# Value products two key tiles at a time, projections between them, in a fused attention and feed-forward kernel

## The reference

```python
x = x + tanh(g_xattn[0]) * linear_attention(layernorm(x), ctx)      # 16 heads of 8
x = x + tanh(g_ffn[0])   * quantised_ffn(layernorm(x))              # 128 -> 512 -> 128
x = x + tanh(g_xattn[1]) * softmax_attention(layernorm(x), ctx)     # 16 heads of 8
x = x + tanh(g_ffn[1])   * experts(layernorm(x))                    # best 2 of 8
...
scores = jnp.einsum('bhqd,bhkd->bhqk', qh, kh) / jnp.sqrt(jnp.float32(D_K))
attn = jax.nn.softmax(scores, axis=-1)
context = jnp.einsum('bhqk,bhkd->bhqd', attn, vh)
...
h = jax.nn.gelu(jnp.einsum('bsd,fed,bske->bskf', x, w1, oh) + b1)
```

## Time and profile before

| | |
|---|---|
| median of 3 runs | 747.04 us (745.25 to 748.69) |
| profiled execution, its own time | 745.49 us |
| its span, first to last instruction | 743.7 us |
| TensorE busy | 665.1 us (89%) |
| VectorE busy | 520.3 us (70%) |
| ScalarE busy | 513.1 us (69%) |
| GpSimd busy | 269.6 us (36%) |

### The profile page before, as it was taken

How to read it: one execution, slowest core, us unless ns; L and a number is a source line. 1 busy time by engine, 2 the same in 40 slices (tenths; PEclk the granted TensorE clock), 3 DMA queues, 4 the chain that set the end, 5 groups by cost and what they waited for, 6 DMA issues and landing times.

```text
span 743.7 us, 19382 instructions
## 1 busy us (share of the span) xinstructions
PE 665.1 (89%) x7302; PEld 467.0 (63%) x7315; DVE 520.3 (70%) x1236; ACT 513.1 (69%) x839; POOL 269.6 (36%) x324
## 2 busy tenths in 40 slices
PE   3499999986468999999999999999999986999997
PEld 3488888874225665666665666566666664577777
DVE  5788989888778779878978878878876751212112
ACT  4488888876326887887787787787887866634441
POOL 4299999992243214304322422432233100000000
PEclk9899999999589999999999999999999999799999
DMA  4122223345523476356537636644664480211110
GB/s 145 41 84 84 83 87 111 111 142 31 121 73 84 98 167 139 95 129 135 130 91 148 149 91 143 135 110 110 135 157 114 86 192 9 60 29 58 29 42 26
DMA packets 59379, 74.42 MB, mean 100 GB/s; under 512 B 35320, under 2 KB 40178, under 8 KB 59306
## 3 DMA queue, kind: packets, MB, share of 16 engines
q1 hardware_dynamic: 59306, 73.39, 41.8%
HBM read 32.35 MB, written 1.40 MB: 45 GB/s over the span
## 4 chain that ended last, share of the span: by engine, by line
PE 43%; DVE 16%; issue 7%; ACT 2%; POOL 2%; SPq 1%; another core or an unknown queue 1%; DMA 1%; DVEq 0%; POOLq 0%; ACTq 0%
DVE mx L1615 8%; PE ps L662 8%; PE ps L750 7%; PE ps L811 7%; PE ps L823 7%; PE ps L737 6%; PE ps L648 4%; PE ps L654 2%; DVE kvall L1446 2%; ACT P L1023 1%; PE ps L684 1%; DVE amax L1485 1%; POOL KP L1134 1%; DVE silu L1530 1%
## 5 line engine op out<-in xcount | busy, mean ns | idle before, releaser
L1023 ACT ACTIVATE P<-ps,kbias,kscale 125x896 f32<-125x896 f32 x192 | 210.3, 1098 | 86.0 <-PE ps L737 83.0
L1615 DVE TENSOR_REDUCE mx<-ps 128x1 f32<-128x500 f32 x336 | 214.0, 671 | 46.6 <-PE ps L662 44.8
L662 PE MATMUL ps<-KP,Qb 128*128 128x500 bf16 x336 | 128.9, 386 | 16.4 <-DVE mx L1615 10.3
L1134 POOL TENSOR_TENSOR KP<-kvall,KP 128x1500 bf16<-128x1500 f32 x16 | 48.6, 3036 | 230.6 <-ACT KP L966 230.6
L750 PE MATMUL ps<-P,Vp 125*32 125x112 f32 x3072 | 113.5, 265 | 2.8 <-ACT P L1023 1.5
L750 PEld LDWEIGHTS ps<-P,Vp 125*32 125x32 f32 x3072 | 67.4, 109 | 53.1 <-issue 37.8
L533 PE MATMUL ps<-wkv,cT 128*125 128x256 f32 x384 | 91.8, 383 | 1.1 <-ACT arena L901 1.1
L533 PEld LDWEIGHTS ps<-wkv,cT 128*125 128x125 f32 x384 | 69.3, 190 | 10.1 <-issue 1.4
L1084 ACT ACTIVATE arena<-ps,b 128x448 f32<-128x448 f32 x64 | 40.4, 633 | 47.4 <-PE ps L811 41.5
L737 PE MATMUL ps<-QS,KS 128*128 128x112 bf16 x768 | 68.8, 215 | 2.4 <-DVE QS L1621 1.4
L737 PEld LDWEIGHTS ps<-QS,KS 128*128 128x128 bf16 x768 | 55.0, 99 | 23.3 <-issue 3.9
(11 more groups left out here) (216 smaller groups left out, 1007.4 us busy)
## 6 DMA issues: line engine op xcount, KB each, us to landing
cT<-ctxT_dram SPq DMA_DIRECT2D x32, 750.0 KB, 4.2
KS<-KP SPq DMA_DIRECT2D x48, 375.0 KB, 7.3
arena<-KP SPq DMA_DIRECT2D x48, 375.0 KB, 7.2
QS<-QD SPq DMA_DIRECT2D x96, 28.0 KB, 5.7
wgu<-w_dram SPq DMA_DIRECT2D x8, 256.0 KB, 3.2
silu<-w_dram SPq DMA_DIRECT2D x8, 256.0 KB, 2.9
x<-xh_dram SPq DMA_DIRECT2D x1, 512.0 KB, 3.6
mixed<-att SPq DMA_DIRECT2D x16, 28.0 KB
```

The costliest lines, as they stand in the source:

```text
L662: ins = nc.tensor.matmul(ps[:, bank, 0:KCW], q[:, 128 * c:128 * c + 128], KP[par][0][:, KCW * k:KCW * k + KCW], start=True, stop=True)
L1023: nc.scalar.activation(P[t % 2][0:TK, :].rearrange("p (k n) -> p k n", k=2), src, ACT.Exp, scale=kscale[0:TK, bass.ds(n, 1)], bias=kbias[0 ...
L1134: nc.gpsimd.tensor_tensor(KP[par][2][:], krest, KP[par][1][:], ALU.subtract).then_inc(sem("kp3_ready"), 1)
L1615: ins = v.tensor_reduce(mx[:, c, k:k + 1], ps[:, bank, 0:KCW], AX.X, ALU.max)
```

## The change

Value products are put off and done for two key tiles together in even tiles (tiles 10 and 11 in the next window's tile 0), except in the last window. The exponentials have four buffers, two of them in a part of `arena` that the first phase has left free. The large projections stand in odd tiles, the small units in even ones. VectorE's steps hang on other MX units; `gate` moves into the next window. At the end, `up` goes over the first half of the rows first, and its first four products and seven of the eight gating products stand between OT, FT, FO and ET.

```diff
+PAT = 6016
 PLACES = [
-    [[["MX0"], ["Q1"], ["MX1"]], [["MX2"], [], ["AT", "MX3"]], [["MX4"], ["OT"], ["MX5"]],
...
+    [[["MX0"], ["Q1"], ["MX1"]], [["MX2"], ["V0"], ["MX3"]], [["MX4"], ["AT"], ["MX5"]],
...
+TOGETHER = 2
...
-        P = [sb(f"P{n}", [128, HQ]) for n in range(2)]
+        P = [sb(f"P{n}", [128, HQ])[:] for n in range(2)]
+        P += [arena[:, PAT + HQ * n:PAT + HQ * n + HQ] for n in range(2)]
...
+                apart = fixed(i) and w == B - 1
...
-                    if t > 0:
+                    if t == 0:
+                        if not first:
+                            for before in range(T - TOGETHER, T):
+                                weigh(w - 1, 1 - par, before, first_pair)
+                    elif apart:
                         weigh(w, par, t - 1, first_pair)
-                    elif not first:
-                        weigh(w - 1, 1 - par, T - 1, first_pair)
+                    elif t % TOGETHER == 0:
+                        for before in range(t - TOGETHER, t):
+                            weigh(w, par, before, first_pair)
...
+            def up(e, par, first, of=range(8)):
+
+                xv = xT[:].rearrange("p (b q) -> p b q", q=HALF)
+                for u in of:
+                    k, c = divmod(u, FC)
...
+            pe.wait_ge(sem("side_free"), emptied((NT - 1, 1), "ET"))
+            up(0, 0, True, range(0, 1))
             fill(AFTER, "OT", B - 1, 1)
-            for unit in LAST:
-                fill(AFTER, unit, NT - 1, 1)
-
-
+            up(0, 0, True, range(1, 2))
+            fill(AFTER, "FT", NT - 1, 1)
+            logits(range(0, 3))
+            fill(AFTER, "FO", NT - 1, 1)
+            up(0, 0, True, range(2, 4))
+            logits(range(3, NT - 1))
+            fill(AFTER, "ET", NT - 1, 1)
             pe.wait_ge(sem("side_free"), emptied(AFTER, "ET"))
...
+            logits(range(NT - 1, NT)).then_inc(sem("logit_ps"), 1)
...
+                    elif par == 0 and k == 0:
+                        pe.wait_ge(sem("logit_ready"), 1)
...
-                if not (first and t < 2):
-                    act.wait_ge(sem("pv_done"), n - 1)
+                if not (first and t < 4):
+                    act.wait_ge(sem("pv_done"), n - 3)
...
-                for unit, later in (("K0", REST_LATER), ("K1", REST_LATER), ("Q1", 2)):
+                for unit, later in (("K0", REST_LATER), ("K1", REST_LATER), ("Q1", 1)):
...
-                        elif unit == "SH":
-                            gate(at, n)
...
-                        if unit == "U":
+                        if unit == "MX0":
+                            gate(prev(at), n)
+                        elif unit == "U":
...
-            lg = ps[:, 6, 0:NT * E].rearrange("p (t e) -> p t e", e=E)
+            lg = ps[:, 4, 0:NT * E].rearrange("p (t e) -> p t e", e=E)
```

More of the change, by code:

```diff
@@ L790, in _ @@
             weigh(B - 1, 1, T - 1, False)
[L791 to L812 removed]
+            def up(e, par, first, of=range(8)):
+                xv = xT[:].rearrange("p (b q) -> p b q", q=HALF)
+                for u in of:
+                    k, c = divmod(u, FC)
+                    if u == 0:
+                        pe.wait_ge(sem(f"w1_in{par}"), loads(e, par))
+                    if not (first and u < 4):
+                        pe.wait_ge(sem("h_ready"), 8 * e + u - 3)
+                    nc.tensor.matmul(ps[:, u % 4, 0:8 * S], w1_sb[par][:, 128 * c:128 * c + 128],
+                                     xv[:, 8 * k:8 * k + 8, 0:S], start=True, stop=True).then_inc(sem("up_ps"), 1)
@@ new lines, in logits @@
+            def logits(tiles):
+                for t in tiles:
+                    ins = nc.tensor.matmul(ps[:, 4, E * t:E * t + E], xT[:, 128 * t:128 * t + 128], gw_sb[:],
+                                           start=True, stop=True)
+                return ins
+            pe.wait_ge(sem("side_free"), emptied((NT - 1, 1), "ET"))
+            up(0, 0, True, range(0, 1))
+            fill(AFTER, "OT", B - 1, 1)
+            up(0, 0, True, range(1, 2))
+            fill(AFTER, "FT", NT - 1, 1)
@@ L838, in second_biases @@
                 ins.then_inc(sem("b2_ps"), 1)
-            up(0, 0, True)
+            up(0, 0, True, range(4, 8))
             def pair2(i):
@@ L1079, in inner @@
                 for u in range(8):
-                    c, k = divmod(u, 2)
+                    k, c = divmod(u, FC)
                     act.wait_ge(sem("up_ps"), 8 * e + u + 1)
@@ L1700, in first_window @@
                             dense(at, n)
-                        elif unit == "MX9":
+                        elif unit == "MX11":
                             first_sum(n)
-                        elif unit == "MX12":
+                        elif unit == "MX14":
                             quantise(n)
-                        elif unit == "MX15":
+                        elif unit == "MX17":
                             quantised(n)
-                        elif unit == "SH":
-                            gate(at, n)
             def second_window(i):
@@ L1735, in second_window @@
                             second_sum(at, n)
-                        elif unit == "MX17":
+                        elif unit == "MX18":
                             normed(n)
```

18 lines of the change are left out of this document (2 added, 16 removed), and 12 rows, old and new, of the table PLACES.

## The result

The changed kernel takes 757.11 us (median of 4 runs, 755.7 to 757.4); the kernel before, run beside it, 747.87 us. The ratio is 1.0122, 95% interval 1.0096 to 1.0147: slower by 1.2%, where 2.3% faster was forecast.

A forecast was written before the change was run, and what follows sets the result against it. TensorE was taken as the bound, VectorE close behind. The terms 14.4 + 2.2 - 1.6 + 2.0 give 17.0 us less: 728.5 from the profiled 745.49, so 730 us against the 747.04 median; range 719 to 741.

The forecast's parts named there:

- The merge: Paired value products in windows 0 to 14: each merge saves TensorE 0.24 us, 1.4 us a window.
- Rival 3: Value products: the merge saves nothing; about 750 us at worst, 745 with evener tiles; chance 5%.
- The evener tiles give back 0.3; of 1.4 us, 1.2 us stay: Attention windows: evenly spaced MX products shrink waits by 0.3 us, so 1.2 of 1.4 us saved a window remain.
- the term of 14.4 us: Twelve attention windows, each 1.2 us shorter: 14.4 us saved.
- (a): SH to the next window's scores: TensorE waits 0.17 or 0.39 us for VectorE's copies, 0.28 on average.
- (b): `gate` moves to the second window's MX0, adding 0.6 to 0.7 us of VectorE's work ahead of MX reductions there.
- (c): `last_normed` behind MX9 in second windows: VectorE comes 0.5 us early for GpSimd's power, TensorE waits some 0.4 at MX12.
- Windows 12 and 13 (+2.2): Windows 12 and 13, without feed-forward chain: 1.1 us saved each, 2.2 us together.
- Window 14 to 15 (-1.6): Window 15's scores wait on a fixed key-transfer chain; later key copy 1.2 us and the pair 0.4 lose 1.6 us.
- The end (+2.0): Last steps: `up` and gating products fill gaps between OT, FT, FO and ET, saving 2.0 us.
- Rival 1: Attention windows: VectorE becomes the bound, 0.6 us a window is left, about 738 us; chance 20%.
- Rival 4: Windows: VectorE's strict order makes TensorE wait 1.9 us in each of 14; slower, 754 us; chance 5%.

The follow-up runs named there:

- second-window anchors and Q1: Changed kernel with second-window hidden-row steps behind MX4 and MX8, last norm behind MX12, and Q1 taken one unit earlier: 744.25 us, ratio 0.9954.
- maxima forward: Against the kernel of second-window anchors and Q1: first-window maxima moved into earlier tiles, `first_sum`, `quantise`, `quantised` behind MX13, MX16, MX19: 735.99 us, ratio 0.9847.
- the two anchors: Against the kernel of maxima forward: first-window `first_sum` behind MX12 (was MX13), `quantised` behind MX18 (was MX19): 730.82 us, ratio 0.9779.
- the way back: Against the kernel of maxima forward: second-window hidden rows behind MX5 and MX9, last norm behind MX13, each one maximum later: 744.36 us, ratio 0.9958.
- The Q1 run: Changed kernel with Q1 taken from bank 6 one unit earlier in tile 0, ahead of MX1's reduction: 753.89 us, ratio 1.0088.
- light maxima: VectorE takes maxima over 250 of 500 columns: the kernel before so edited 732.76 us (ratio 0.9786), the changed kernel so edited 739.36 us (0.9890).
- the run with moved anchors: Changed kernel with `quantise` and `quantised` behind MX12 and MX16, hidden rows behind MX4 and MX8, last norm behind MX12: 756.58 us, ratio 1.0117.
- the OT run: Changed kernel, first windows with OT in tile 2, AT in 4, DE in 6, `first_sum` and quantising behind MX14, MX16, MX18: 766.54 us, ratio 1.0272.
- the run of three together: Changed kernel with OT, AT, DE turned round, second-window anchors at MX4, MX8, MX12, and Q1 one unit earlier: 752.02 us, ratio 1.0074.

## Why the prediction was wrong

**The merge (0.24 us each, 1.4 a window): right for TensorE's own work.** 0.90 us for two against 0.52 for one, and the work without waits fell by 1.2 us in a first and 1.1 in a second window. Rival 3 (it saves nothing) is out, though in the changed kernel new waits took more than it saved.

**"The evener tiles give back 0.3; of 1.4 us, 1.2 us stay": this step failed, and with it the term of 14.4 us.** I counted the tiles' length on TensorE, about 2 us each, and took that for even work on VectorE. Between the engines lie only banks 4 and 5, and VectorE's steps have fixed places among the maxima. The change put five of seven of them between the halves of a two (two of seven before), and crowded those of first windows into tiles 5 to 9 while VectorE idled in tiles 0 to 4. Instead of 1.2 us gained, a first window lost 1.5 and a second 0.15. That it was the places and not the amount is shown by runs that only move: second-window anchors and Q1 (-12.9 us against the changed kernel), maxima forward (another -8.3), the two anchors (another -5.2, part of it by shorter steps beside GpSimd), and the way back (+8.4 for one maximum's shift in second windows). The step failed for the pairs by themselves too: in the old places they lost 0.8 and 0.7 us a window. The merge does give 16.9 us in the places that were found for it, and the forecast had 14.4 + 2.2; that the two are close is luck, since the second is measured against single products in places that do not suit them. Against the kernel before with the new end the pairs gain 7.9 us there, and 13.0 after the last anchors were moved.

**Bank 6, not in the prediction.** A small unit stands directly ahead of a large projection, and both use the one side bank. TensorE stands 0.59 us for it at V0 and 0.49 at V1 in a steady first window. The Q1 run shows the first (3.2 us); the second stayed open, since taking the late copy away brought a wait of about the same size a tile on.

**Give-back (a), SH to scores: right.** The scores come 1.87 us after SH (412.75) and waited 0.26 (0.28 forecast on average); VectorE's copies had ended at 414.51. **(b) `gate`: wrong in sign.** Moving it back costs 0.8 us a second window; the total of that run moved by less than the noise. **(c) `last_normed`: right in kind**, but VectorE waits 0.15 us for GpSimd, not 0.5. TensorE's row for (a):

```profile
414.62 0.36 PE L740 MATMUL ps<-QS,arena 128*128 128x112 bf16 x4 [0.26 <-issue]
```

VectorE's row:

```profile
427.80 0.35 DVE L1684 TENSOR_SCALAR xe<-x,mv,rstd 128x128 f32 x1 [0.15 <-POOL rstd L1205]
```

**Windows 12 and 13 (+2.2): wrong.** Window 12 is 23.62 us (23.70 before), 13 is 26.13 (25.03). The forecast had a fixed chain only for window 14, and it binds here too: ScalarE's second half of the keys starts 6.80 us into window 12 (5.60 before, the 1.2 us later that the prediction had for window 14), and the scores of window 13 wait 1.66 us for the transfers. **Window 14 to 15 (-1.6): right in place, about 1.0 in size.** From the SH of window 13 to the scores of window 15 it is 0.63 us more than before, and the pair of 0.4 us now follows the wait. The wait itself is 3.49 us against 2.59:

```profile
623.21 0.57 PE L740 MATMUL ps<-QS,arena 128*128 128x112 bf16 x8 [3.49 <-DMA QS<-QD]
```

**The end (+2.0): right as far as it can be told.** From the last `weigh` to the first `down` it is 27.20 us in the kernel before, 24.84 in the run with the end alone and 24.62 in the changed kernel: 2.4 to 2.6 us less. The medians give 3.8, with an interval from 2.0 to 5.8; single executions differ by 2 us, for a reason told below of window 15. The gating products now run at the higher level of the clock: six records in 0.73 us, where sixteen took 3.58:

```profile
641.78 1.02 PE L810 MATMUL ps<-xT,wgu 128*128 128x448 f32 x2
...
642.96 0.73 PE L816 MATMUL ps<-gw_sb,xT 128*128 128x8 f32 x6
...
650.46 11.76 PE L810 MATMUL ps<-xT,wgu 128*128 128x448 f32 x24 [2.81 <-ACT arena L1105]
```

The last row is the limit that was forecast: `up` 4 waits for ScalarE, 2.81 us. The granted clock was 1.00 from 641.8 to 646.4 us, over the fillers, and 0.55 behind that wait, from 650.4 to 656.

**The rivals.** Rival 1 (VectorE full, 738) had the right engine and the wrong quantity: with light maxima both kernels gain, and the changed one stays behind. Rival 4 (slower, by VectorE's strict order, from 1.4 us of waits a window on) is what happened, at 757 instead of 754 us, with new waits of 2.7 us in first and 1.2 in second windows. It had been given 5%, and that its time is near is partly luck: `gate` was no cost at all, and `last_normed` waited 0.15 us for GpSimd; it was one of three steps whose places cost 1.35 us a second window together. The Trainium skill (TensorEngine Tiling (Array Packing), PSUM Bottleneck) warns that, once tiling has made TensorE faster, the emptying of PSUM may become the bottleneck. The trace agrees as far as the waits are for VectorE's emptying: 24.1 us over the span, 10.3 before. It adds that the cure here was the order, at the same amount of emptying: 16.7 us in the run of 735.99.

## What to carry to other kernels

Before short products are merged, write down when the engine behind them gets its next piece and where its own long steps stand: with two banks in between, a step belongs behind the last piece of a group, never between its pieces, and the gap that the merge makes is where it fits. A timeline in which that engine idles in one half of a loop and never pauses in the other shows where pieces should go; moving three steps by one place cost 8.4 us here, where the whole change cost 9.2. And a unit should not stand directly ahead of another that uses the same single buffer.

## What the runs showed of the hardware

**Waits can cost twice.** In the run with moved anchors TensorE stood 1.63 and 1.22 us within 4.3 us, and the granted clock behind it was 0.52, the 1.2 GHz level, for about 3 us:

```profile
403.00:407.20 4.20, 2.02 (x12) 0.81 (x10) 3.56 (x11) 1.60 (x2) 4.08 (x6) 1.00 1.05 215
407.20:410.40 3.20, 2.53 (x27) 1.78 (x31) 2.95 (x7) 1.40 (x3) 0.80 (x3) 0.52 1.01 181
```

An MX product took 0.60 us there instead of 0.39. The same shows in the OT run, where a pair took 1.72 us instead of 0.97 behind waits of 1.68 and 0.96, at a clock of 0.50. In the changed kernel's steady windows the waits are shorter and the clock is 1.00.

The same wait does not always bring the clock down. Ahead of window 15 TensorE stands 2.59 us for the transfers in the profiled execution of the kernel before, and 2.60 us in that of the run with the new end alone, which has the same windows. The 16 us around it, first in the kernel before, then in that run (the third number from the end is the granted clock):

```profile
605.99:613.99 8.00, 5.20 (x100) 4.05 (x98) 2.04 (x7) 4.50 (x8) 0.74 (x2) 1.00 0.76 184
613.99:621.99 8.00, 7.62 (x175) 5.59 (x174) 0.99 (x5) 7.21 (x7) 0.00 (x0) 1.00 0.01 2
```

```profile
606.00:614.00 8.00, 5.40 (x81) 4.19 (x74) 2.18 (x8) 3.87 (x6) 0.22 (x2) 0.78 0.80 195
614.00:622.00 8.00, 7.66 (x149) 5.74 (x146) 1.00 (x5) 5.80 (x6) 0.52 (x1) 0.79 0.01 2
```

From SH to the last `weigh` window 15 took 19.8 us at the one and 22.1 at the other. So 2.3 us of one execution's time can hang on this alone.

**VectorE's addition of two fp32 operands beside GpSimd.** `key_rest` lasts 0.67 us, but 1.75 in the run of three together, while GpSimd made `Qb`. The two engines' timelines there:

```profile
402.66 0.68 DVE L1636 TENSOR_REDUCE mx<-ps 128x1 f32<-128x500 f32 x1
403.26 1.75 DVE L1467 TENSOR_TENSOR kvall<-kvall,KP 128x500 f32<-128x500 f32 x1
```

```profile
402.79 1.69 POOL L1169 TENSOR_TENSOR Qb<-QP,hmask 128x896 bf16<-128x896 bf16 x1
```

The addition ends 0.53 us after `Qb`; the reduction out of PSUM just ahead of it, 0.68 us, was not lengthened. The Trainium skill (SBUF — State Buffer, SBUF: two separate sides) says that the two engines share a pair of ports, that a VectorE operation with two SBUF inputs needs it, and that whoever comes second is blocked for the other's whole instruction. The trace agrees with that: the addition that came second ends later than the end of the other by little less than it lasts alone. So a step's place in time has a price on this side too.
